# Expert tiles of 256 tokens for 384, tokens turned once and copied to both halves: one kernel on one core

## What is computed

```python
x = x + conv_ref(ln_c(x), ...)
t = to_tokens(x)
t = t + ffn_ref(ln_t(t), Wg, bg, W1, b1, W2, b2)
x = from_tokens(t, x)
```

```python
top_w, top_i = jax.lax.top_k(xf @ Wg + bg, 2)
top_w = softmax(top_w)
for e in range(8):
    h = gelu(xf @ W1[e] + b1[e])
    out = out + w_dense[:, e:e+1] * (h @ W2[e] + b2[e])
```

## Time and profile before

| what | value |
|---|---|
| median of 3 runs | 2283.13 us (2280.98 to 2287.26) |
| the profiled execution's own time | 2289.27 us |
| its span, first to last instruction | 2287.5 us |
| mean granted clock of TensorE over the span | 0.915 |
| PE busy | 1959.1 us, 86% |
| VectorE (DVE) busy | 1456.3 us, 64% |
| GpSimd (POOL) busy | 972.4 us, 43% |
| ScalarE (ACT) busy | 785.5 us, 34% |
| expert stage, first load to merge's first load | 1543.9 to 2212.2 us |

### The profile page before, as it was taken

The page is one execution under the profiler, slowest core; times in us unless marked ns, Lnnn a source line. Parts: engine busy times, 40 slices in busy tenths (PEclk is TensorE's granted clock), DMA queues, the critical chain, the costliest instruction groups (busy, mean ns, idle before and its releaser), DMA issues. The chain is left out here.

```text
span 2287.5 us, 34748 instructions
## 1 busy us (share of the span) xinstructions
PE 1959.1 (86%) x11630; PEld 1105.3 (48%) x11630; DVE 1456.3 (64%) x2524; ACT 785.5 (34%) x1382; POOL 972.4 (43%) x1038
## 2 busy tenths in 40 slices
PE   8985898787989999999999984408999999999955
PEld 5652444344555545555555544304555555555534
DVE  4444566565878977989779886624555555555534
ACT  4431111111223223232232322305556666666620
POOL 8001000100224351443514537764777777777740
PEclk9987999898999999999999995559999999999976
DMA  9767888887888787887888733236666666566439
GB/s 289 165 135 184 203 199 208 205 193 200 210 204 218 212 208 206 229 217 206 215 209 223 217 98 112 64 87 158 165 157 168 169 161 163 156 169 167 109 114 357
DMA packets 265829, 419.09 MB, mean 183 GB/s; under 512 B 116224, under 2 KB 188452, under 8 KB 242685
## 3 DMA queue, kind: packets, MB, share of 16 engines
q1 hardware_dynamic: 160701, 348.14, 57.6%
q0 software_dynamic: 32352, 39.58, 6.6%
q10 hardware_dynamic: 72608, 29.25, 5.4%
HBM read 337.34 MB, written 89.60 MB: 187 GB/s over the span
## 5 line engine op out<-in xcount | busy, mean ns | idle before, releaser
L951 POOL DMA_INDIRECT token_rows<-gate_rows,gate_index x392 | 414.5, 1057 | 662.2 <-DVE gate_index L1280 548.5
L1158 DVE TENSOR_TENSOR prod<-z_ps,r_all 119x896 f32<-119x896 f32 x512 | 542.7, 1083 | 126.3 <-PE z_ps L1071 100.9
L1473 POOL DMA_INDIRECT mixed<-exp_mix,exp_xt x474 | 479.8, 1012 | 193.2 <-issue 154.2
L1075 PE MATMUL z_ps<-xq,band 112*119 112x448 f32 x1024 | 438.1, 563 | 70.5 <-DVE prod L1158 70.4
L1491 ACT ACTIVATE exp_hid<-exp_h_ps,exp_pack 128x384 f32<-128x384 f32 x632 | 329.7, 574 | 263.0 <-PE exp_h_ps L1529 263.0
L1075 PEld LDWEIGHTS z_ps<-xq,band 112*119 112x119 f32 x1024 | 181.5, 186 | 277.0 <-issue 174.2
L1529 PE MATMUL exp_h_ps<-exp_tok,exp_pack 64*128 64x384 f32 x1264 | 247.5, 510 | 0.0
L984 ACT ACTIVATE ob<-o_ps 128x448 f32<-128x448 f32 x64 | 34.8, 544 | 601.8 <-PE o_ps L1088 601.8
L1088 PE MATMUL o_ps<-prod,pick 119*32 119x448 f32 x2048 | 238.6, 559 | 1.2 <-DVE prod L1158 0.3
L1537 PE MATMUL exp_y_ps<-exp_hid,exp_pack 128*64 128x384 f32 x1264 | 230.9, 486 | 0.0
L1571 DVE COPY exp_tok<-exp_x_ps 128x384 f32<-128x384 f32 x158 | 88.1, 557 | 223.6 <-PE exp_x_ps L1516 219.5
(11 more groups left out here) (195 smaller groups left out, 2051.8 us busy)
## 6 DMA issues: line engine op xcount, KB each, us to landing
xq<-xs SPq DMA_DIRECT2D x192, 896.0 KB
exp_pack<-packs SPq DMA_DIRECT2D x158, 258.5 KB
exp_xt<-token_rows SPq DMA_DIRECT2D x158, 120.0 KB
xs<-xpad SPq DMA_DIRECT2D x32, 448.0 KB, 5.9
co<-ob ACTq DMA_DIRECT2D x64, 224.0 KB, 16.2
xin<-in_x_dram SPq DMA_DIRECT2D x8, 1568.0 KB, 11.9
merge_yt<-mixed ACTq DMA_DIRECT2D x28, 448.0 KB, 6.4
mixed<-exp_mix,exp_xt POOLq DMA_INDIRECT x474
```

The lines of the kernel that those rows point to most:

```text
L951: pool.indirect_dma_start(out=token_rows[:, :], out_offset=bass.IndirectOffsetOnAxis(ap=index[b % RR][:, j:j + 1], axis=0), in_=rows[b % R ...
L1075: mm = nc.tensor.matmul(zt, band[t % BR][rows_in, at:at + MF], maps, start=True, stop=True)
L1158: nc.vector.tensor_tensor(prod[(NU * t + u) % PR][:, :, :].rearrange("p m (d x) -> p m d x", d=D), z_ps[(NU * t + u) % 3][0:MF, :, 0:CN].r ...
L1473: pool.indirect_dma_start(out=mixed[:, :], out_offset=bass.IndirectOffsetOnAxis(ap=xt[t % XT][:, j, ROW_ID:ROW_ID + 1].bitcast(U32), axis= ...
```

## The change

TILE_BLOCKS goes from 3 to 2, so that a tile has 256 tokens, there are 223 tiles, two scatters per tile, and matmuls, activations and VectorE's instructions of the expert stage have 256 columns. The sums of x and convolution move from every fifth to every seventh step. The turn is one transpose per block of 128 tokens, into the upper 64 partitions of PSUM alone; VectorE copies this to the upper half of the tile of tokens, and copies that half from SBUF to the lower half, for which hidden waits.

```diff
-TILE_BLOCKS = 3
+TILE_BLOCKS = 2
-    sum_at = {5 * d + 4: d for d in range(DUAL)}
+    sum_at = {7 * d + 4: d for d in range(DUAL)}
+        tok_again = sem("tok_again")
                 for j in range(TILE_BLOCKS):
-                    for e in range(2):
-                        mm = nc.tensor.matmul(x_ps[C * e:C * (e + 1), P * j:P * (j + 1)],
-                                              xt[t % XT][:, j, 0:C], ident[:, :], start=True, stop=True)
+                    mm = nc.tensor.transpose(x_ps[0:C, P * j:P * (j + 1)], xt[t % XT][:, j, 0:C], ident[:, :])
                 mm.then_inc(turned, 1)
             def hidden(t, hb):
                 if hb == 0:
-                    pe.wait_ge(tok_done, t + 1)
+                    pe.wait_ge(tok_again, t + 1)
-                nc.vector.tensor_copy(tok[t % 3][:, :], x_ps[:, 0:N]).then_inc(tok_done, 1)
+                nc.vector.tensor_copy(tok[t % 3][0:C, :], x_ps[0:C, 0:N]).then_inc(tok_done, 1)
+                dve.wait_ge(tok_done, t + 1)
+                nc.vector.tensor_copy(tok[t % 3][C:P, :], tok[t % 3][0:C, :]).then_inc(tok_again, 1)
```

## The result

The changed kernel took **2405.12 us** (median of 4 runs, 2398.33 to 2409.16), beside 2283.99 us for the kernel before: ratio 1.0525, 95% interval 1.0501 to 1.0549. It is 5% slower; 2265 had been forecast, in a range of 2240 to 2290. The profiled execution took 2398.33 us.

The account below looks back on a forecast made before the run. PE bounds the kernel before; after the change SP's issues would, at 19.72 us per seven tiles, then PE at 2.70 a tile. With a shorter tail, merge starts 18.1 us earlier: 2283.1 becomes 2265, range 2240 to 2290.

Parts of the forecast that it names:

- the part on SP: Load queue in the expert stage: issues need 613 us against PE's 602, 19.72 us per seven tiles; scatter waits mostly go.
- the sum: Whole kernel: 27 rounds of seven tiles at 19.72 us, 30 tiles at 2.70, then 17.7 to merge, 18.1 us earlier.
- Rings of nine and six buffers: Expert-stage load buffers: they cannot hide SP's queue, too slow on average at 2.82 us a tile.
- DMA: Expert-stage loads: 16.8 MB more, share 0.61 to about 0.73; loads land a little later, without slowing the kernel.
- SP's pace: Main case for the expert stage: SP's issues set 2.82 us a tile while base and conv load; chance 0.50.
- Merge's first load: End of the expert stage: 17.7 us from the last tile's hidden to merge, in place of 22.85.
- PE's tile: TensorE in the expert stage: 2.68 to 2.78 us a tile, taken as 2.70; hidden 1.07, outputs 0.97, turns 0.32 to 0.37 each.
- PE's pace: Rival for the expert stage: PE still sets the pace at 2.70 us a tile, 2243 us in all; chance 0.15.
- Changing over: Rival on PE: more stage changes, or queues waiting in turn, make 2.85 to 2.90 us a tile, 2276 to 2287; chance 0.22.
- the three queues hold each other up: Half of a rival: SP, PE and GpSimd, at 95% and over, wait in turn, 2.85 to 2.90 us a tile; joint chance 0.22.
- The port: Rival: VectorE's added copy holds up GpSimd's scatters, 2.95 us a tile, 2297 us; chance 0.13.
- The signs: Expert-stage trace: SP still waiting 50 us or more for scatters would prove the forecast wrong, with PE or GpSimd leading.

Follow-up runs that it names:

- run 8: Kernel before the change with six token-row buffers in place of nine, nothing else: 2960.89 us.
- run 1: Changed kernel with fifteen token-row buffers in place of nine: 2280.92 us in one execution.
- run 3: Changed kernel with the same base and conv loads on SP spread, one or two per step: 2301.72 us.
- run 6: Changed kernel with SP issuing the pack of a tile ahead of the token rows of two tiles later: 2329.55 us.
- run 11: Changed kernel, nine row buffers, without base and conv loads after the first step, so part of the output is not computed: 2271.41 us.
- run 12: Changed kernel with fifteen token-row buffers, timed again over seven executions: 2265.97 us, ratio 0.9960 to the kernel before.
- run 9: Changed kernel with fifteen token-row buffers and base and conv sums at every eighth tile in place of every seventh: 2255.53 us, ratio 0.9904 to the kernel before.
- run 4: Changed kernel with tokens turned twice on PE and copied once by VectorE, as before the change: 2414.08 us.
- run 7: Changed kernel with fifteen row buffers and the next tile's pack issued ahead of the rows of two tiles later: 2286.42 us, ratio 0.9999 to the kernel before.

## Why the prediction was wrong

- **The step that failed** is in the part on SP: "SP's wait for the scatters of seven tiles back mostly goes, since SP comes to it later; what is late next is the pack". It stayed, 140.7 us of it. The prediction took SP as a rate, 19.72 us of issues against 18.90 of PE, and let the difference of 0.8 us be all that is late per seven tiles. But the wait for scatters ties SP to the pipe: a shorter tile shortens the seven tiles in the loop by 7 x 1.28 = 8.9 us and the loop itself by only 5.2. Of 5.2 us to spare 1.5 are left, and a burst now needs 3.2 of them in place of 1.9 (run 8). Measured it is 3.40 us a tile over the whole of hidden's stretch, where the sum had SP's 2.82. The row for it was at hand, 163.5 us of waits: read as free time that the change could take, it was the sign of a loop that closes with little to spare. That wait told how long SP was held, not how early its loads were.
- "Rings of nine and six buffers cannot hide a queue that is too slow on average" was right and not what mattered: neither can they hide a burst when the wait holds the queue back to the ring's length. Runs 1, 3, 6 and 11 each loosen one of the three (ring, burst, order), and each takes most of, or half of, the loss away.
- **No term for the clock.** The sum held PE's idle time at its length. Most stalls of some 3 us bring work at half clock behind them, so that 86 us of idle before hidden go with a loss of 135.
- **DMA.** "Room is left, and loads land a little later, which shifts and does not slow" holds for the mean, a share of 0.58 over hidden's stretch, and not behind a burst: slow landing is some 12 of the 83 us of stalls, and in runs 3 and 6 three quarters and half of the stalls that are left.
- The sums of single parts held. SP's pace of 2.82 us a tile is what rules once the ring is long: 2.84 measured in run 12. Merge's first load came 14.7 us after the last hidden (2322.72), forecast 17.7. Copies of 417 and 287 ns stand for 426 and 296, GpSimd, given 2.65 us a tile, was not the limit and waited for VectorE (214.3 us). PE's tile came to 2.787 for 2.70: hidden 1.07 and turn 0.34 were met, outputs took 1.01 for 0.97 and the turn back 0.37, the upper of its two bounds. The 2.70 was taken nearer the lower end, and the upper one, 2.78, was it. Under SP's 2.82 this cost nothing.
- **The rivals.** PE's pace (2243): out of reach at 2.787 us a tile, though run 9 shows PE ruling, at 2255.5. Changing over: an undisturbed tile of 2.787 us is short of its 2.85. Its other half, "the three queues hold each other up", is the nearest that the prediction came; it had neither the loop nor its size, 2.85 to 2.90 us a tile for 3.40. The port: falls with run 4. The scatters' median is 983 ns as before. That also answers the Trainium skill, "SBUF — State Buffer", section "SBUF: two separate sides", by which the added copy and a scatter would shut each other out for a whole instruction: the copy's median is 287 ns and its longest 591, so a hold of 0.3 us is seen at times, and none of 0.98. Of the 223 copies 109 start while a scatter runs, 69 of them with more than 0.3 us of it still to come, and these 69 take no longer than 0.30 us. Where page and runs differ, the runs decide.
- The signs were named rightly ("SP still waiting 50 us or more for scatters"), but read as "then PE or GpSimd leads". It was neither: a loop through all of them led. No case of the prediction had that loop, and so none lay near 2405.

The Trainium skill, "DMA: Bandwidth & Descriptors", section "Anatomy of one DMA — SWDGE (gpsimd) path", states that DMA engines do not wait on semaphores, any wait happening on the issuing sequencer before dispatch. The trace agrees: in run 8 the rows of tile 67 go at 2080.88, the next, which wait for scatters, only at 2093.75, and a pack whose own buffer had long been free goes 1.15 us behind these: the wait is SP's, and holds all that SP has still to issue.

## What to carry to other kernels

For a queue that issues loads in order, work out two numbers: its rate, and the loop from a load to the event that frees its buffer. Count the loop in tiles up to the load that stands *behind* the waiting one, take it from that many tiles of time, and hold what is left against what the longest burst in the queue takes beyond a tile; here a smaller tile took 8.9 us from this product, 5.2 from the loop, and made the burst dearer by 1.3. Enlarge the ring or spread the burst together with such a change, and then see whether the rate still fits.

## What had not been expected of the hardware

- After 3.0 us without matmuls TensorE came back at a granted clock of 0.50 and stayed there for about six microseconds of work (1907.2 to 1913.3), after which it was 1.00 again. Not every stall does this: after 2.53 us without matmuls hidden took its usual 1.13 us at 1932.35, and the granted clock stayed at 1.00 (1929.0 to 1935.0). In run 8, where PE stands for some 6.9 us before every other tile, its granted clock over 100 us is 0.80.
- Loads of one queue took very different times: 2.7 us for the pack of 258.5 KB in the stall shown, up to 5.7 us for such a pack right behind a burst (run 6), 5.5 us for the rows of 80 KB behind a burst and a pack (run 7). The DMA engines' mean share says little about it: it was 0.6 to 0.8 over most of run 7's expert stage, and 0.95 in these ten microseconds:

```profile
1763.00:1773.00 10.00, 8.22 (x60) 4.41 (x58) 5.78 (x15) 7.10 (x19) 7.64 (x8) 1.00 0.95 235
```
